# The residual add of the attention-output stage, moved from VectorE to GpSimd

## The reference

```python
x = x + _layernorm(_L0_attn_ref(_layernorm(x, axis=-1), Wq, bq, Wk, bk, Wv, bv, Wo, bo), axis=-1)
x = x + _layernorm(_L0_ffn_ref(_layernorm(x, axis=-1), weight, w_scale, bias), axis=-1)
...
# _L0_ffn_ref
absmax = jnp.max(jnp.abs(x), axis=-1, keepdims=True)
scale = jnp.maximum(absmax, eps) / 127.0
q = jnp.clip(jnp.round(x / scale), -128, 127).astype(jnp.int8)
acc = jnp.einsum('bsk,nk->bsn', q, weight, preferred_element_type=jnp.int32)
out = acc.astype(jnp.float32) * in_scale * w_scale[:, 0] + bias
```

## Time and profile before

| | us |
|---|---|
| median of two runs | 4080.23 |
| lowest and highest | 3999.13, 4161.33 |
| the profiled execution's own time | 3997.97 |
| its span on the slowest core (core 7) | 3996.4 |
| spans of all eight cores | 3977.3 to 3996.4 |
| TensorE busy, over the span | 2620.1 |
| VectorE busy | 1104.0 |
| ScalarE busy | 1095.3 |
| GpSimd busy | 152.0 |

### The profile page before, as it was taken

The page is one execution under the profiler, slowest core; times in us unless marked ns, Lnnn a source line. Parts: engine busy times, 40 slices in busy tenths (PEclk is TensorE's granted clock), DMA queues, the critical chain, the costliest instruction groups (busy, mean ns, idle before and its releaser), DMA issues.

```text
span 3996.4 us, 33753 instructions; the slowest of 8 cores (3977.3 to 3996.4 us)
## 1 busy us (share of the span) xinstructions
PE 2620.1 (66%) x11368; PEld 1141.7 (29%) x11368; DVE 1104.0 (28%) x1897; ACT 1095.3 (27%) x1714; POOL 152.0 (4%) x44
## 2 busy tenths in 40 slices
PE   0000019999787778887778887778957787436544
PEld 0000004444333333433333433333422333112221
DVE  0006201111033322233322233322233555302112
ACT  0003200000045334545333445433441222101111
POOL 0000000000000000000000000000000000003323
PEclk9999999999888889988889988889977778667777
DMA  9998880010200111100111100011014333443332
GB/s 130 130 176 287 219 151 37 37 42 37 67 18 12 27 27 27 27 18 9 27 27 27 27 19 14 22 27 27 6 63 143 105 126 116 123 88 94 86 84 95
DMA packets 351211, 282.25 MB, mean 71 GB/s; under 512 B 321090, under 2 KB 321090, under 8 KB 337474
## 3 DMA queue, kind: packets, MB, share of 16 engines
q1 hardware_dynamic: 273220, 204.59, 17.5%
q0 software_dynamic: 3072, 41.94, 7.7%
q10 hardware_dynamic: 74752, 33.57, 3.5%
HBM read 191.92 MB, written 117.44 MB: 77 GB/s over the span
## 4 chain that ended last, share of the span: by engine, by line
PE 52%; DVE 11%; ACT 9%; another core or an unknown queue 7%; ACTq 5%; DMA 5%; issue 4%; POOL 4%; SPq 4%; DVEq 0%; POOLq 0%
PE ps_b L362 11%; PE ps_v L264 11%; PE ps_b L380 6%; PE ps_b L523 6%; PE ps_b L528 6%; PE ps_b L481 5%; ACTq L803 4%; PE ps_c L702 3%; ACT P_sb L492 3%; DVE bn6b L638 2%; DMA xln_h<-xlnb 2%; DVE t L410 2%; SPq L220 2%; ACT kT L370 2%
## 5 line engine op out<-in xcount | busy, mean ns | idle before, releaser
L492 ACT ACTIVATE P_sb<-ps_b,negb 128x512 bf16<-128x512 f32 (+3 forms) x1280 | 686.4, 642 | 108.3 <-PE ps_b L481 106.1
L523 PE MATMUL ps_b<-P_sb,v_sb 128*128 128x512 bf16 (+3 forms) x1280 | 460.0, 360 | 64.5 <-DVE P_sb L500 50.8
L264 PE MATMUL ps_v<-wv_all,xT 128*128 128x512 bf16 x2048 | 445.1, 381 | 46.2 <-DMA wv_all<-wv_r 46.2
L362 PE MATMUL ps_b<-xT,wkh 128*128 128x512 bf16 x2048 | 447.2, 380 | 23.1 <-DMA wkh<-wk_bf 23.1
L528 PE MATMUL ps_b<-P_sb,ones_sq 128*128 128x512 bf16 (+3 forms) x1280 | 454.6, 360 | 0.0
L481 PE MATMUL ps_b<-qT,kT 128*128 128x512 bf16 (+3 forms) x1280 | 429.6, 364 | 6.6 <-DVE negb L456 6.6
L824 PE MATMUL ps_c<-big,qTj 128*128 128x512 bf16 x1024 | 241.1, 401 | 286.9 <-DMA qTj<-q_h 286.9
L236 PE MATMUL ps_v<-bv_sb,ones_f 1*128 1x512 f32 x8 | 7.2, 1069 | 533.8 <-DMA xT<-xln_h 533.8
L380 PE MATMUL ps_b<-xT,wqh 128*128 128x512 bf16 x1024 | 259.1, 421 | 81.0 <-ACT kT L370 81.0
L264 PEld LDWEIGHTS ps_v<-wv_all,xT 128*128 128x128 bf16 x2048 | 201.1, 98 | 291.4 <-issue 51.6
L362 PEld LDWEIGHTS ps_b<-xT,wkh 128*128 128x128 bf16 x2048 | 199.9, 98 | 263.5 <-issue 27.1
(11 more groups left out here) (75 smaller groups left out, 1640.2 us busy)
## 6 DMA issues: line engine op xcount, KB each, us to landing
xin<-x_seq SPq DMA_DIRECT2D x48, 1024.0 KB, 7.9
xln_h<-xlnb ACTq DMA_DIRECT2D x32, 512.0 KB, 8.4
v_nat<-vout SPq DMA_DIRECT2D x32, 512.0 KB, 2.6
v_sb<-v_nat SPq DMA_DIRECT2D x512, 32.0 KB, 1.9
x_h<-x1b SPq DMA_DIRECT2D x16, 1024.0 KB, 3.9
x1c<-x_h SPq DMA_DIRECT2D x16, 1024.0 KB, 7.8
out<-att SPq DMA_DIRECT2D x16, 1024.0 KB, 4.7
wq_bf<-wq_r POOLq DMA_DIRECT2D x1, 8192.0 KB, 88.4
```

The costliest lines, as they stand in the source:

```text
L264: tmm = P.do("tensor", lambda t, par=par, kc=kc, ncc=ncc, st=st: t.matmul(ps_v[:, par * 4 + ncc, :], xT[:, kc, st * 128:(st + 1) * 128], w ...
L362: tmm = P.do("tensor", lambda t, par=par, kc=kc, nc8=nc8: t.matmul(ps_b[:, nc8, :], wkh[:, par, kc, :], xT[:, kc, nc8 * 512:(nc8 + 1) * 51 ...
L492: t_e = P.do("scalar", lambda sc, i2=i2, qoff=qoff: sc.activation(P_sb[:, i2, qoff:512], ps_b[:, i2, qoff:512], AF.Exp, bias=negb[:, :], s ...
L523: P.do("tensor", lambda t, par=par, kt=kt, qcp=qcp, qoff=qoff, first=first, is_last=is_last, i2=i2: t.matmul(ps_b[:, 4 + qcp, qoff:512], v ...
```

## The change

The residual add of C1 is issued on GpSimd instead of VectorE, with the same operands and the same waits, and it counts up `gg` instead of `vv`.

```diff
-                t_x1[j] = P.do("vector", lambda v, j=j, jp=jp: v.tensor_tensor(
+                t_x1[j] = P.do("gpsimd", lambda g, j=j, jp=jp: g.tensor_tensor(
                     x1b[:, jp, :], wrk[:, :], xin2[:, jp, :], ALU.add),
-                    after=dep_x1 + [t_ln2], sem="vv")
+                    after=dep_x1 + [t_ln2], sem="gg")
```

## The result

| | us |
|---|---|
| predicted | 4019.0 (3998 to 4047) |
| with the change, median of 11 runs | 4019.08 |
| before, median of 10 runs | 4000.6 |
| ratio, after to before | 1.0048, 95% interval 1.0036 to 1.0061 |
| profiled execution, before and after | 3997.97, 4017.41 |

Of the two runs behind the 4080.23 given ahead one was a slow one, in which the cores of one die or of both show a lower granted clock, as 4 of the 10 and 4 of the 11 are here; the ratio is taken from the others alone, whose medians are 3997.7 and 4017.4 us. The kernel is slower by 19.7 us, half a per cent, clear of noise and within the 2% band.

The account below looks back on a forecast made before the run. The prediction took C1 to be paced by a chain of tail, SP, load and TensorE burst holding nine of the 16 adds. Nine tails at 2.34 us, 21.1 us, on 3997.97 gave 4019 us, range 3998 to 4047.

Parts of the forecast that it names:

- The seven others must remain hidden: C1's seven tails off the chain: their growth costs nothing, as VectorE keeps 3.7 us of idle time, before 6.07.
- "nothing" at which TensorE was costed: Second matmul burst of each C1 round: gap grows to some 2.7 us, burst stays 21.0 us, no cost.
- What bounds C1: C1: no engine is full; a chain of tail, SP, load and TensorE burst paces it, 54.5 us per two tiles.
- What goes, what comes: C1's add: VectorE's 2.29 us turn into idle time, and GpSimd takes 4.51 us for the same add.
- both far ends of the bound: Limits for the GpSimd add's length: 2.29 us, as fast as VectorE, to 9.15 us, both GpSimd operations of a C2 tile.
- The handovers: Semaphore waits around the add: +0.06 us before GpSimd starts, +0.06 on ScalarE's line 733, giving 2.34 us per tail.
- On the path or beside it: C1's 16 tails: nine on the chain pay in full, 9 x 2.34 = 21.1 us; the other seven pay nothing.
- The count of nine tails: Adds on C1's chain: seven rounds with one each, the first, and the last tile's; each pays 2.34 us.
- C2 and the stores: C2 only moves, unchanged at 455 us; the x1 store, issued 2.3 us later, moves no load; no cost.
- Hidden anyway: Rival: TensorE sets C1's pace, so the add's length doesn't count; 3998 us, chance 0.06.
- All 16 tails pay: Rival: VectorE's spare time vanishes, C1's tails follow without a gap; 4035 us, up to 4067 with a slower add; chance 0.07.
- The clock staying low: Rival: the added 2.3 us gap keeps TensorE's first bursts at 1.2 GHz, 10.8 us more each; 4105 us, chance 0.04.

Follow-up runs that it names:

- e5: Kernel before, add still on VectorE, each tile's four yTj loads issued one tail earlier, ahead of the stores: ratio 0.9906, C1 403.5 us.
- e2: Kernel before with the add moved to GpSimd for odd tiles 1 to 13 only: ratio 1.0035, C1 455.9 us.
- e8: Kernel before with only the odd tiles' loads issued early and the add on GpSimd for tiles 1 to 13 odd: ratio 1.0001, C1 442.6 us.
- e3: Kernel before with the add moved to GpSimd for the even tiles and tile 15 only: ratio 1.0053, C1 461.4 us.
- e4: The changed kernel with the GpSimd add issued three times in a row in each tail: ratio 1.0368 to the kernel before, C1 588.4 us.
- e6: The changed kernel, add on GpSimd, with all yTj loads issued one tail earlier: ratio 0.9991 to the kernel before, C1 439.9 us.
- e9: The changed kernel with the GpSimd add in four 512-column instructions, each bn_stats waiting only for its quarter: ratio 1.0010 to the kernel before, C1 444.8 us.
- e11: Kernel before with loads issued one tail earlier and the add split by columns, half on VectorE, half on GpSimd: ratio 0.9897, C1 400.3 us.
- e10: The changed kernel with the GpSimd add in four quarters and loads issued one tail earlier: ratio 0.9918 to the kernel before, C1 409.8 us.

## Why the prediction was right, and where it was wrong

Two steps failed, "The seven others must remain hidden" and the "nothing" at which TensorE was costed. The runs showed in their place a second loop over the odd tiles that had 2 to 3 us to spare and not 6, and bursts that grow slower when the gap ahead of them grows. That the number came out near is in part luck.

*What bounds C1.* Right in its main point: a chain of tail, SP, load and burst, not an engine. e5 confirms it by cutting it.

*What goes, what comes.* Right. VectorE's 2.29 us turned into waiting, GpSimd took 4.49 us (4.51 forecast) for the three-buffer form, so both far ends of the bound fell away. The Trainium skill's 4497 ns for this form (GPSIMD Engine Reference, section "Elementwise — side-by-side cycle accounting"), which the sum did not use, is met by the trace: 4.49 us.

*The handovers.* 2.28 us per tail instead of 2.34, for the add takes 0.02 us less than forecast and starts 0.26 us after ScalarE, not 0.30. Over nine tails this is 0.5 us.

*On the path or beside it.* Here a step failed: "The seven others must remain hidden", with 3.7 us of VectorE's idle time as their cover. e2 shows the seven costing 14.4 us by themselves, and e8 shows them costing nothing once no load waits for an odd tail. VectorE's 6.07 us of waiting were taken for time that tail j+1 had to spare. But that tail's end releases the load of tile j+3, and TensorE was waiting for it: the earlier trace rows has that row, with 0.33 us and the load as releaser. The wait was read as small, and it was the sign that this loop had little to spare either: its load, burst and tail take 51.5 us of the round, so 3 us are left on core 7 and not 6. The chain of core 3 before runs over the odd tiles in its second half, and the prediction followed the chain of core 7 alone. The count of nine tails came out usable because with the change the tails of both loops grow by the same amount, so whichever loop is the longer, the growth is paid once per round and not twice: the chains of the changed kernel hold eight or nine adds of GpSimd, and on at least six of the eight cores they change over from even to odd tiles before the last one. The forecast's "3.7 us of idle time" for VectorE and its 2.7 us gap for TensorE both fell with this step.

*TensorE.* "I cost it at nothing", with a gap near 2.7 us and a burst of 21 us, was wrong in both numbers. From tile 5 on the gaps are 5.7 us ahead of even bursts and 4.2 ahead of odd ones in the mean of all cores (8.1 and 1.3 before), and the odd bursts take 22.7 us, where they took 21.2. Granted clock (the column before the last two) of the burst that starts at 3262.26 on core 3:

```profile
3262.30:3266.30 4.00, 4.00 (x5) 1.76 (x6) 0.69 (x4) 2.26 (x2) 0.23 (x1) 0.50 0.20 82
3266.30:3269.40 3.10, 3.10 (x5) 0.71 (x4) 0.00 (x0) 0.00 (x0) 3.10 (x1) 0.50 0.00 0
3269.40:3272.00 2.60, 2.60 (x8) 0.94 (x8) 1.23 (x2) 0.00 (x0) 1.17 (x1) 0.50 0.24 101
```

It starts at 0.50, 1.2 GHz, behind 3.39 us of gap and stays there for all of the 9.7 us shown. Over all eight cores, from TensorE's timelines, 57 bursts before came behind a gap of under 2 us and took 20.8 us in the mean, and 37 came behind more than 8 us and took 23.3. With the change 77 came behind gaps of 3.5 to 6.5 us and took 22.8. So each loop now has bursts of about 22.8 us, where one had 23.3 and the other 20.8. For the pacing loop that is up to 0.5 us less per round, 3.5 us over seven rounds; counted by tile instead, even bursts went from 23.3 only to 23.1, which is 1.4 us. What is missing is 21.1 - 0.5 - 17.9 = 2.7 us, so the size fits, but no more. e3, whose gaps still alternate (1 and 12 us in the mean), has a C1 2.0 us longer than the change's with only nine of the adds; its pacing bursts take 23.2 us, so they explain less than half of that. No run changed the gaps alone: this share is argued and not shown.

*C2 and the stores.* Right within 1 us: 449.9 and 448.8 us.

*The rivals.* "Hidden anyway" fell. "All 16 tails pay" is no rival to the change as it is, but it is what happens in e4, e5 and e6, and its point of decision, two tails against one round, is right. The clock staying low did not happen in the way described (slower first bursts); the second bursts are the ones that became slower. The agreement of 4019.0 with 4019.08 is luck: over the runs on which the ratio rests the median is 4017.4. The forecast for C1 was 3.2 us too high, and the time of the whole program, which is that of its slowest core, grew by 19.7 us, 1.8 more than C1 did in the mean of the cores; nothing in the forecast stood for that.

## What to carry to other kernels

Idle time on an engine is not slack of the instructions ahead of it: ask what their end releases, and whether anybody waits for that, even if only for 0.3 us. Where two buffers make two interleaved loops, write down the round of each; where both are near their limit, as here, slowing down one costs nearly as much as slowing down both. The cure was to cut the dependence that closes them (a load queued behind a store on the same issuing queue, worth 38 us), and it is worth looking for before any operation is moved. Moving work to an idle engine helps only if the old engine has other work to do in that time or the new one runs beside it, as the quarters of e9 do.

## What the runs showed of the hardware that had not been expected

- An add on GpSimd with two SBUF inputs and one on VectorE with two SBUF inputs exclude each other almost fully (e11: 2.34 against 3.40 us, 1.23 against 3.09), while bn_stats on VectorE, with one input, leaves GpSimd alone: the 64 quarters took 1.25 to 1.28 us each, on every core of e9 and e10.
- Splitting an add on GpSimd costs little: four quarters take 4.92 us in a row, one whole add 4.49, so 0.14 us for each further instruction.
- A burst on TensorE takes longer behind a short gap, so the gap costs more than its own length. In e2, the 17 bursts of all cores behind a gap of under 0.6 us took 20.5 us in the mean, the 21 behind 2 to 3.5 us took 22.4, and behind more than 8 us it was 23.2.
